# Edge lists loaded and indexed one stage earlier, and blank rows written by plain transfers

## What is computed

```python
def _L0_gnn_ref(h, weight, edge_src, edge_dst, edge_rel, edge_norm):
    msg = h[edge_src] * edge_norm[:, None]
    seg = edge_rel * N + edge_dst
    agg = jax.ops.segment_sum(msg, seg, num_segments=R * N).reshape(R, N, NUM_BASES, SUBMAT_IN)
    W = weight.reshape(R, NUM_BASES, SUBMAT_IN, SUBMAT_OUT)
    return jnp.einsum('rnbi,rbio->nbo', agg, W).reshape(N, NUM_BASES * SUBMAT_OUT)

def _L1_ffn_ref(x, Wg, bg, W1, b1, W2, b2):
    _, idx = jax.lax.top_k(x @ Wg + bg, 2)
    mask = jax.nn.one_hot(idx, E, dtype=x.dtype).sum(axis=-2)
    h = jax.nn.gelu(jnp.einsum('td,edh->teh', xf, W1) + b1[None], approximate=False)
    y = jnp.einsum('teh,ehd->ted', h, W2) + b2[None]
    return jnp.einsum('ted,te->td', y, mf)

x = x + _L0_gnn_ref(_layernorm(x, axis=-1), L0_gnn_weight, src, dst, edge_type_8, edge_weight)
# feed-forward of half the nodes, attention over the edges
x = x + _L1_ffn_ref(_layernorm(x, axis=-1)[None], ...)[0]
```

## Time and profile before

| | |
|---|---|
| median of 3 runs | 6659.32 us |
| profiled execution, its time | 6661.88 us |
| profiled execution, its span | 6660.2 us |
| busy: TensorE, weight loads, VectorE, ScalarE, GpSimd | 71%, 60%, 60%, 30%, 64% |
| stage 1: last store of the table issued | 377.33 us |
| stage 2: first and last gather start | 398.30, 2489.60 us |
| stage 10: first instruction | 5781.27 us |
| stage 11: first instruction | 5816.30 us |

### The profile page before, as it was taken

One profiled execution on the slowest core, in us unless ns is written; L12 is line 12 of the kernel. 1 busy time (PEld: TensorE's weight loads), 2 busy tenths in 40 slices (PEclk: granted clock), 3 DMA queues, 4 the chain that ended last, 5 costly groups with the idle time before them and its releaser, 6 DMA issues. The chain is left out here.

```text
span 6660.2 us, 114468 instructions
## 1 busy us (share of the span) xinstructions
PE 4699.2 (71%) x25073; PEld 4027.4 (60%) x25073; DVE 3979.9 (60%) x11855; ACT 1984.7 (30%) x4950; POOL 4287.4 (64%) x4672
## 2 busy tenths in 40 slices
PE   9955555555555558599377777676776667499997
PEld 4435555555555556599255655555655557499996
DVE  5565555555555559522577777777777768544442
ACT  3310000000000006133144444444444434266664
POOL 1257777777777777255677777777777738644443
PEclk9987777777777779699677677777777775599998
DMA  7853333333333339111444444444444435344445
GB/s 291 319 179 105 104 105 104 104 104 104 104 104 105 104 101 302 49 64 63 147 114 113 114 113 113 114 113 114 114 114 113 113 120 183 131 71 72 71 71 128
DMA packets 374944, 810.50 MB, mean 122 GB/s; under 512 B 88930, under 2 KB 232882, under 8 KB 361044
## 3 DMA queue, kind: packets, MB, share of 16 engines
q0 software_dynamic: 210480, 527.37, 29.8%
q1 hardware_dynamic: 136660, 158.51, 7.5%
q10 hardware_dynamic: 27568, 122.44, 5.0%
HBM read 578.58 MB, written 242.27 MB: 123 GB/s over the span
## 5 line engine op out<-in xcount | busy, mean ns | idle before, releaser
L1252 POOL DMA_INDIRECT s_rows<-xp_table,s_index x1664 | 1654.3, 994 | 507.4 <-issue 456.7
L327 POOL DMA_INDIRECT s_rows<-rel_table,s_staged x1664 | 1585.2, 953 | 535.3 <-issue 494.5
L356 PE MATMUL s_part<-s_pick,s_rows 128*128 128x128 f32 x6656 | 1205.9, 355 | 915.8 <-DMA s_rows<-rel_table,s_staged 712.2
L356 PEld LDWEIGHTS s_part<-s_pick,s_rows 128*128 128x128 f32 x6656 | 1117.4, 262 | 1004.8 <-DVE s_pick L364 967.1
L1376 PE MATMUL s_part<-s_pick,s_scaled 128*128 128x128 f32 x6656 | 1411.9, 369 | 369.7 <-DVE s_scaled L1541 347.2
L1376 PEld LDWEIGHTS s_part<-s_pick,s_scaled 128*128 128x128 f32 x6656 | 1182.0, 260 | 568.2 <-issue 284.1
L377 DVE TENSOR_TENSOR sums<-sums,s_part 128x256 f32 x1666 | 702.7, 422 | 932.9 <-PE s_part L356 747.3
L1556 DVE SCALAR_TENSOR_TENSOR sums<-sums,s_old_share,s_part 128x256 f32 x1666 | 792.3, 476 | 429.0 <-PE s_part L1376 291.1
L1288 ACT ACTIVATE s_apart<-window,s_local 128x128 f32<-128x128 f32 x1664 | 531.7, 390 | 1132.5 <-PE s_part L1376 1071.3
L1541 DVE TENSOR_TENSOR s_scaled<-s_rows,s_share 128x256 f32<-128x256 f32 x1664 | 686.7, 413 | 77.7 <-issue 76.6
L364 DVE TENSOR_SCALAR s_pick<-window,s_local,s_weight 128x128 f32<-128x128 f32 x1669 | 641.9, 385 | 14.1 <-issue 0.2
(11 more groups left out here) (358 smaller groups left out, 5435.5 us busy)
## 6 DMA issues: line engine op xcount, KB each, us to landing
rel_table<-s_rows ACTq DMA_DIRECT2D x98, 1024.0 KB
s_rows<-exp_rows SPq DMA_DIRECT2D x212, 132.0 KB, 2.1
s_rows<-rel_table,s_staged POOLq DMA_INDIRECT x1664
s_rows<-xp_table,s_index POOLq DMA_INDIRECT x1664
s_edges<-edge_rows SPq DMA_DIRECT2D x208, 80.0 KB
xp_table<-s_xp ACTq DMA_DIRECT2D x49, 264.0 KB, 3.9
s_x<-in_x SPq DMA_DIRECT2D x98, 128.0 KB, 4.1
s_x<-in_x SPq DMA_DIRECT2D x49, 256.0 KB
```

The lines of the kernel that those rows point to most:

```text
L327: pool.indirect_dma_start(out=rows[:, s, :], out_offset=None, in_=rel_table[:, :], in_offset=bass.IndirectOffsetOnAxis(ap=staged[:, 2 * s ...
L356: mm = pe.matmul(part[s % PARTS][:, k, :], rows[:, s, k * P:(k + 1) * P], pick[:, s % PICKS, :], start=True, stop=True)
L1252: pool.indirect_dma_start(out=rows[:, b * BATCH + s, :], out_offset=None, in_=xp_table[0:NP, :], in_offset=bass.IndirectOffsetOnAxis(ap=in ...
```

## The change

**Edge lists.** The buffers `first`, `index`, `local` and `weight` now exist from before stage 1 until the end of stage 2. Ends, chunk firsts, sources and odd firsts have a buffer of stage 1, `raw`, instead of lying in `rows`. SP issues the seven transfers in stage 1, behind the loads of tiles 0 and 1 and ahead of the loop with the other loads. VectorE computes `index` and shifts the odd words behind its eviction of tile 96, and `local` and the pair words behind that of tile 97. In stage 2 SP has nothing left, ScalarE doesn't wait before it stages, GpSimd waits for `staged` alone, and VectorE starts with its clearings.

**Blank rows.** `fill` is now one word for each expert, the row where its rows end. SP waits for three steps of `filled`, reads the word of each expert into a register and issues one plain transfer of 256 rows, eight in all, and waits for them. GpSimd issues nothing.

```diff
@@ stage 1, SP @@
                     load(0, 0, 0)
                     load(1, 0, 1)
+                    sp.dma_start(index[:, :], a["type_chunk"]).then_inc(edges_in, 16)
+                    sp.dma_start(source, a["src_chunk"]).then_inc(edges_in, 16)
+                    sp.dma_start(ends, a["dst_chunk"]).then_inc(edges_in, 16)
+                    sp.dma_start(chunk_first, a["dst_chunk"][0:1, :].broadcast_to([P, CHUNKS])).then_inc(edges_in, 16)
+                    sp.dma_start(odd[0:1, :], a["dst_chunk"][0:1, :]).then_inc(edges_in, 16)
+                    sp.dma_start(first[:, 1:CHUNKS // 2 + 1], a["dst_first"][0:1, 1:SPANS + 1]).then_inc(edges_in, 16)
+                    sp.dma_start(weight[:, 0:CHUNKS], a["weight_chunk"]).then_inc(edges_in, 16)
                     with sp.Fori(0, PAIRS - 1) as i:
@@ stage 1, VectorE @@
                         evict(t, i, b)
+                        if left == 1:
+                            gather_index()
+                            odd_up()
+                        if not left:
+                            local_ends()
+                            pair_nodes()
@@ stage 2, ScalarE and GpSimd @@
-                    act.wait_ge(index_done, 1)
                     stage(0, 0)
                     stage(0, 1)
...
                         pool.wait_ge(staged_done, b + 1)
-                        if b == 1:
-                            pool.wait_ge(edges_done, 2)
-                            pool.wait_ge(pairs_done, 2)
@@ stage 2, VectorE: the operations that were here are the bodies of the four functions above @@
-                    v.wait_ge(edges_in, 16 * 7)
-                    v.scalar_tensor_tensor(out=index[:, :], in0=source, scalar=float(R), in1=index[:, :],
-                                           op0=ALU.mult, op1=ALU.add).then_inc(index_done, 1)
-                    v.tensor_tensor(local[:, 0:CHUNKS], ends, chunk_first, ALU.subtract).then_inc(edges_done, 1)
...
                     v.memset(sums[:, :, :], 0.0).then_inc(cleared, 1)
@@ stage 10, SP @@
+                    sp.wait_ge(filled, 3)
+                    for e in range(X):
+                        row = sp.value_load(fill[0:1, e:e + 1], min_val=0, max_val=X * CAP - 2 * P)
+                        sp.dma_start(exp_rows[ds(row, 2 * P), :].rearrange("(k p) d -> p k d", p=P), blank[:, :, e, :]).then_inc(zeros_out, 16)
+                    sp.wait_ge(zeros_out, 16 * X)
                     sp.wait_ge(left_over_out, 32)
@@ stage 10, GpSimd and VectorE @@
-                    pool.wait_ge(filled, 4)
-                    for k in range(2):
-                        for e in range(X):
-                            pool.indirect_dma_start(out=exp_rows[:, :], in_=blank[:, k, e, :], in_offset=None,
-                                                    out_offset=bass.IndirectOffsetOnAxis(ap=fill[:, k, e:e + 1], axis=0)).then_inc(zeros_out, 16)
-                    pool.wait_ge(zeros_out, 32 * X)
...
-                    for k in range(2):
-                        v.tensor_scalar(fill[:, k, :], count[:, :], line[:, :], float(k * P), ALU.add, ALU.add).then_inc(filled, 1)
+                    v.tensor_copy(fill[:, :], count[:, :]).then_inc(filled, 1)
```

More of the change, by code:

```diff
@@ L150, in gnn_kernel @@
         end_stage()
+        wp_of = ExitStack()
+        wp = at(wp_of, "wp", [P, HALVES, EXT])
+        sums_of = ExitStack()
+        sums = at(sums_of, "sums", [P, HALVES, NP + P])
+        gather_of = ExitStack()
+        first = at(gather_of, "s2_first", [1, CHUNKS // 2 + 1], I32)
+        index = at(gather_of, "s2_index", [P, CHUNKS], I32)
+        local = at(gather_of, "s2_local", [P, CHUNKS + AHEAD])
+        weight = at(gather_of, "s2_weight", [P, CHUNKS + AHEAD])
         with ExitStack() as st:
@@ L155, in gnn_kernel @@
             xt = at(st, "s1_x", [P, 2, D])
+            raw = at(st, "s1_raw_edges", [P, 4, CHUNKS], I32)
+            ends, chunk_first, source, odd = (raw[:, k, :] for k in range(4))
+            edges_in, pairs_done, edges_done = sem("s1_edges_in"), sem("s1_pairs_done"), sem("s1_edges_done")
             stat = at(st, "s1_stat", [P, 2, 6])
@@ L269, in gnn_kernel @@
         end_stage()
-        wp_of = ExitStack()
-        wp = at(wp_of, "wp", [P, HALVES, EXT])
-        sums_of = ExitStack()
-        sums = at(sums_of, "sums", [P, HALVES, NP + P])
         with ExitStack() as st:
-            first = at(st, "s2_first", [1, CHUNKS // 2 + 1], I32)
-            index = at(st, "s2_index", [P, CHUNKS], I32)
-            local = at(st, "s2_local", [P, CHUNKS + AHEAD])
-            weight = at(st, "s2_weight", [P, CHUNKS + AHEAD])
             rows = at(st, "s2_rows", [P, SLOTS, D])
@@ L282, in gnn_kernel @@
             pick = at(st, "s2_pick", [P, PICKS, P])
-            later = rows[:, SLOTS // 2:SLOTS, :].rearrange("p s d -> p (s d)").bitcast(I32)
-            ends, chunk_first, source, odd = (later[:, k * CHUNKS:(k + 1) * CHUNKS] for k in range(4))
             part = [bank(st, f"s2_part{k}", HALVES, P) for k in range(PARTS)]
-            edges_in, index_done, edges_done, pairs_done, cleared = sem("s2_edges_in"), sem("s2_index_done"), sem("s2_edges_done"), sem("s2_pairs_done"), sem("s2_cleared")
+            cleared = sem("s2_cleared")
             staged_go, staged_done, gather_go = sem("s2_staged_go"), sem("s2_staged_done"), sem("s2_gather_go")
@@ L394, in _ @@
                     v.sem_inc(added, PARTS - 2)
[L395 to L398 removed]
+                    v.wait_ge(cleared, 6)
                     for c in range(LOOK):
@@ L410, in gnn_kernel @@
         end_stage()
+        gather_of.close()
         with ExitStack() as st:
@@ L2133, in gnn_kernel @@
             line = at(st, "s10_line", [P, 1])
-            fill = at(st, "s10_fill", [P, 2, X], I32)
+            fill = at(st, "s10_fill", [P, X], I32)
             row_i = at(st, "s10_row_i", [P, 2, X], I32)
```

35 lines of the change are left out of this document (15 added, 20 removed).

## The result

| | before | changed |
|---|---|---|
| median of the runs | 6658.75 us (6654.48 to 6664.19, 6 runs) | 6629.19 us (6622.55 to 6630.06, 6 runs) |
| profiled execution | 6661.88 us, span 6660.2 | 6630.06 us, span 6628.2 |

The ratio is 0.9955, with an interval of 0.9945 to 0.9965: 23 to 37 us less, 29.6 by the medians. The forecast was 25.3 less (6634.0 us, range 6628 to 6642). So the change is faster, as forecast, and the size forecast lies inside the interval, 4.3 us short of the difference of the medians.

The account below looks back on a forecast made before the run. TensorE was taken to set the table stage's pace, GpSimd's gathers to bound the relation pass, and GpSimd's 16th indirect transfer to be stage 10's last wait. −14.9 + 2.0 − 12.4 = −25.3 us gave 6634.0 us, range 6628 to 6642.

Parts of the forecast that it names:

- Part 1: Start of the relation pass: with the index ready at the barrier, the first gather comes 14.9 us earlier, at 383.4.
- products come 23 us earlier: Relation pass: clearing of `sums` ends at 403.5 instead of 426.7, so products start 23 us earlier, with 16 slots filled.
- Part 2: Table's stage: tile 2's load lands behind the edge lists in SP's queue, so its transposes start 2.0 us later.
- TensorE has no idle time in the rest of the stage, so all of it stays: Table's stage: the 2.0 us by which tile 2 is late remain until the stage's end.
- Part 3: Stage 10, blank rows: eight plain transfers by SP replace sixteen indirect ones by GpSimd, ending 12.4 us earlier.
- with the same 2.8 us: Stage 10: from the last blank transfer's landing to the next stage 2.8 us pass, as before, giving 5804.0.
- VectorE's chain is late next: Stage 10: VectorE's chain, ending at 5799.50, is what becomes late next, 1.7 us below the transfers.
- The bytes are hidden: Answers a table's stage rival: edge lists push the stores, costing 13.3 us instead of 2.0; 6645.3 us, chance 0.06.
- Blank rows do gain: Answers a stage 10 rival: plain transfers cost 2.7 us each, so nothing is gained there; 6646.4 us, chance 0.04.
- GpSimd was not held by the clearing: Answers a relation pass rival: VectorE's clearing delays gathers to 403.5, 5.2 us later than before; 6654.1 us, chance 0.02.
- The gathers' pace: Relation pass rival: VectorE and GpSimd operations collide, 41 ns on each of 1664 gathers, 68.2 us; 6702.2 us, chance 0.03.
- clearing at 384: Relation pass, a sign to look for: the clearing of `sums` stands at 384 us.

Follow-up runs that it names:

- c1: The kernel before, unchanged, run again for a second trace; 6659.49 us.
- e2: The kernel before with only the blank rows changed, edge lists still loaded in stage 2; 6645.38 us against 6660.91, ratio 0.9975.
- e1: The changed kernel without the blank rows' change, so only the edge lists are moved; 6643.7 us against 6660.91 for the kernel before, ratio 0.9975.
- c2: The changed kernel, unchanged, on the chip where the kernel before takes 7973.21 us; 7934.43 us, ratio 0.9949.
- c3: The changed kernel, unchanged, run beside e9; 6637.97 us against 6667.29 for the kernel before, ratio 0.996.
- e5: The changed kernel with the eight blank transfers shared by SP and ScalarE, four each; one run on the slower chip, 7928.32 us.
- e6: The changed kernel with sixteen plain blank transfers of 128 rows from SP instead of eight of 256; 7944.69 us against 7970.05 for the kernel before.
- e7: The changed kernel with three of four index operations ahead of VectorE's last eviction and `sums` cleared in two halves; one run on the slower chip, 7956.0 us.
- e3: The changed kernel with ScalarE instead of SP issuing the seven edge lists, once tile 0 has landed; 6625.7 us against 6660.91 for the kernel before, ratio 0.9946.
- e8: The changed kernel with the edits of e4 and e5 together; 7944.68 us against 7973.21 for the kernel before, ratio 0.9955.
- e9: The changed kernel with tiles 2 and 3 loaded between SP's second and third list, blank rows as in e5; 6634.24 us against 6667.29 before, ratio 0.9951.
- e4: Against e3: ScalarE's function table loads before the lists, and the last three lists follow its first eviction; one run on the slower chip, 7955.21 us.

## Why the prediction was right, and where its terms were off

**Part 1, −14.9 for the first gather: right.** From the last store to the first gather it was 398.30 − 377.33 = 20.97 us, and is 385.47 − 379.30 = 6.17: 14.8 less. The steps hold too. No wait followed: clearing begun before the gathers, first products at 412 behind it, run of the gathers unchanged within its scatter. One sum of this part was wrong without cost. It took the clearing for its row of 21.18 us and let the products come 23 us earlier. The whole clearing is 26.4 us (see the hardware below), and the first one-hot matrix came at 411.85 instead of 427.46 us, 15.6 earlier, beside gathers that came 12.8 earlier; 21 of the 64 slots were taken by then, not 16.

**Part 2, +2.0: the mechanism right, the term too small.** That tile 2 lands behind the lists was right (they moved from 7.6 to 18.2 us, where 8 to 18.4 was forecast), and so was its size: TensorE takes tile 2 up at 19.51, 18.93 and 19.65 us in the three traces of the old order (before, c1, e2) and at 21.11 to 21.62 in seven of the new one (changed, e1, c2, c3, e5, e6, e7), 2.0 us later in the mean. What failed is the step "TensorE has no idle time in the rest of the stage, so all of it stays": more than all stayed. The last store was at 377.33, 376.7 and 377.2 in the old order, 377.1 in the mean; in the new one at 379.3, 380.1, 380.8, 380.8, 380.9, 381.2 and 381.2, 380.6 in the mean, so **3.5 us and not 2.0**. The sum had priced the late start and not the clock behind the pause:

- pause of 1.73 us (changed) and 1.66 (c2): eight products in 3.60 us;
- pause of 2.19 to 2.97 (e1, c3, e5, e6, e7): eight products in 4.85 to 5.30 us, so 1.3 to 1.7 more, with a granted clock of 0.50 to 0.54 in the lower of the stretches 21 to 23 and 23 to 25 us.

The slower products are 1.1 us in the mean of the seven, out of the 1.5 us that were missing; the other 0.4 are not traced. What the pauses differ by is when TensorE is through with tile 1, whose eight products took 4.08 and 4.42 us in the first two traces and 3.60 to 3.77 in the other five. The profiled run of the changed kernel fell on the cheap side of that, so the result alone would have shown the term as right (1.97 us). The other traces correct it: −14.8 + 3.5 = −11.3, where I had −12.9.

**Part 3, −12.4: right in kind, 1.8 us too careful.** 14.2 us in the changed kernel, in e2 and in c3. The spacing was right (1.14 for 1.19 forecast, 0.3 us less over the seven steps), and e6 confirms that issues are the price. The first issue came 0.6 us later in the stage than forecast (5773.32 − 5763.68 = 9.64 us against 5790.3 − 5781.27 = 9.03). The step that failed is "with the same 2.8 us", which put 2.6 us to landing and 2.8 on to the next stage, 5.4 in all, behind SP's last issue. It was 5784.61 − 5781.30 = 3.3. The 2.8 was the rest of GpSimd's 5.2 us from its last transfer to stage 11, and I had carried it over to another engine and another kind of transfer with no row for it. So 0.6 − 0.3 − 2.1 = −1.8 us. VectorE's chain is late next, as the prediction said, and e5 shows that 1.8 us are left above it.

**The sum.** Terms as the traces give them: −14.8 + 3.5 − 14.2 = −25.5, against −25.3 forecast. Two errors of 1.5 and 1.8 us cancelled, so that the sum comes out within 0.2 us is luck. The medians say −29.6, and −29.3 for c3; the intervals hold 25.5. Whether the other 4 us are real, no run settles. The gathers' run scatters by 5.3 us between executions of one kernel (2085.7 and 2091.0 in the changed one). On the other hand the medians of e1 and e3 too lie 6 and 8 us beyond what their traces explain, and that of e2, with the lists late, only 1.3: a further gain of the early lists, at a place that these traces don't show, is not excluded.

**Rivals.** The bytes are hidden (DMA share 0.96 in the hole; e8, e9 and e4 show that what reaches beyond it costs 1.3 to 2.3 us at the last store, not 13.3). Blank rows do gain. GpSimd was not held by the clearing: the second and all later gathers from 387.00 on take 0.95 while it runs. The Trainium skill (SBUF — State Buffer, section "SBUF: two separate sides") says that a VectorE operation in a two-port mode keeps GpSimd from writing descriptors; the 19 gathers that start from 387.00 to 409.51 show nothing of the kind for this clearing, as the trace of before had suggested. Where VectorE does seem to hold GpSimd is stage 10 of the kernel before (e6). The gathers' pace did not change.

## What to carry to other kernels

A DMA hole at the start of a stage is a place for loads that a later stage waits for, but count what is queued behind them on their engine and which stores they meet: whichever order was tried here, 1.3 to 3.5 us of the price stayed. Many small transfers in a stage in which nothing else runs are paid by the issue, so merge them before moving them to another engine. And a tail taken from one engine's last transfer must not be carried over to another's: bound it instead.

## What the runs showed of the hardware

- A pause of TensorE can cost more than its length: behind 2.2 to 3.0 us of idling (five traces) the granted clock fell to 0.5 and eight products cost 1.3 to 1.7 us more; behind 1.2 to 1.7 us (e4, c2 and the changed kernel) they did not. In c2 and the changed kernel TensorE had also come to full pace later (tile 1's products, above), so the length of the pause is not shown to be the only cause.
- A long clearing's row is drawn shorter than the work. The whole is one row of 21.18 us behind 5.26 of "issue"; in e7 its halves are rows of 10.62 with 2.6 of "issue" ahead of each, and from the small clearings to the first picks it is 27.19 us both times (384.66 to 411.85, 386.17 to 413.36). The idle time is in proportion to the size, so it belongs to the operation: about 26.4 us, begun at 384.8. The prediction's "clearing at 384" is right, though the row shows 390.03.
- GpSimd's indirect transfers take 0.97 us in stage 10 of the kernel before, and 1.87 and 2.31 beside two operations of VectorE with two inputs; a reduction and the clearing beside them did not lengthen them.
- On the second chip both edge passes are slower in all six traces taken there (first to last gather of the relation pass 2494 to 2498 us instead of 2085 to 2091), and the kernel before takes 7970 us instead of 6660, while the table's stage and stage 10 are as elsewhere. Its traces show pauses of about 6 us on TensorE for which no releaser is named; their cause is open.
